# Graph network kernel: TensorE's addresses of a group in one row, read by one load behind the last sum

## What is computed

```python
deg = maximum(segment_sum(ones, dst, n), 1)          # first network, 3 steps
for _ in range(3):
    msg = silu(concat([h[src], h[dst], edge_attr]) @ W1e + b1e) @ W2e + b2e
    agg = segment_sum(msg, dst, n) / deg
    h = h + silu(concat([h, agg]) @ W1n + b1n) @ W2n + b2n
x = layernorm(x + h)
for W, root, b in layers:                            # second network, 3 layers, relu between
    seg = edge_type * n + dst
    agg = segment_sum(h[src], seg, 4 * n) / maximum(count, 1)
    h = h @ root + b + einsum('rni,rio->no', agg, W)
out = layernorm(x + h)
```

## Time and profile before

| | us |
|---|---|
| median of 3 runs | 6185.32 |
| lowest, highest | 6181.42, 6193.58 |
| profiled execution | 6186.73 |
| its span | 6184.7 |
| busy in it: TensorE, DVE, POOL, ACT | 4992.0, 3707.7, 3328.4, 2689.5 |

### The profile page before, as it was taken

How to read it: one execution, slowest core, us unless ns; L and a number is a source line. 1 busy time by engine, 2 the same in 40 slices (tenths; PEclk the granted TensorE clock), 3 DMA queues, 4 the chain that set the end, 5 groups by cost and what they waited for, 6 DMA issues and landing times.

```text
span 6184.7 us, 171993 instructions
## 1 busy us (share of the span) xinstructions
PE 4992.0 (81%) x47650; PEld 4584.0 (74%) x47651; DVE 3707.7 (60%) x9362; ACT 2689.5 (43%) x4966; POOL 3328.4 (54%) x4176
## 2 busy tenths in 40 slices
PE   3666666631888888888888888889999999999998
PEld 2444444421777776888878888879998999989997
DVE  6444444421777775555545555478885888768885
ACT  1111111112556565555545555555553555545553
POOL 1777777740555553444434444446663666636663
PEclk9999965555899998999989999999997999989997
DMA  8111111148899995666646666624442444324441
GB/s 311 29 29 29 29 29 29 29 117 260 282 291 305 301 305 188 220 221 220 221 153 224 221 222 221 201 92 132 132 132 72 133 133 132 128 79 133 132 132 58
DMA packets 358208, 975.40 MB, mean 158 GB/s; under 512 B 70911, under 2 KB 83539, under 8 KB 358154
## 3 DMA queue, kind: packets, MB, share of 16 engines
q1 hardware_dynamic: 317096, 946.00, 46.4%
q0 software_dynamic: 38400, 28.13, 2.6%
q10 hardware_dynamic: 2658, 0.51, 0.0%
HBM read 774.54 MB, written 199.05 MB: 157 GB/s over the span
## 4 chain that ended last, share of the span: by engine, by line
PE 67%; POOL 14%; issue 11%; DMA 4%; another core or an unknown queue 2%; DVE 2%; ACT 0%; POOLq 0%; SPq 0%; ACTq 0%; DVEq 0%
PE sums L902 20%; PE sums L897 15%; POOL recs L510 13%; PE gat L871 11%; PE gat L872 11%; PE gat L875 6%; DMA arena<-recs 2%; DMA recs<-arena 2%; PE gat L994 1%; PE gat L992 1%; PE sums L1005 1%; DVE arena L1149 0%; PE gat L794 0%; PE gat L976 0%
## 5 line engine op out<-in xcount | busy, mean ns | idle before, releaser
L523 POOL TENSOR_SCALAR arena<-iota_f,arena 128x128 f32<-128x128 f32 x1920 | 1210.5, 647 | 1471.1 <-PE sums L897 1285.2
L871 PE MATMUL gat<-table,arena 128*128 x7680 | 1945.3, 254 | 28.6 <-issue 12.8
L872 PE MATMUL gat<-table,arena 128*128 x7680 | 1945.5, 254 | 0.0
L902 PE MATMUL sums<-arena 128*128 128x192 bf16 x15360 | 1887.1, 246 | 0.0
L1293 DVE TENSOR_SCALAR arena<-iota_s,meta_t 128x512 bf16<-128x512 int16 x3840 | 1525.5, 470 | 360.6 <-PE sums L902 360.6
L897 PE MATMUL sums<-arena 128*128 128x64 f32 (+1 forms) x7680 | 1020.3, 278 | 414.1 <-issue 410.4
L902 PEld LDWEIGHTS sums<-arena 128*128 128x128 bf16 x15360 | 1325.2, 98 | 0.1
L897 PEld LDWEIGHTS sums<-arena 128*128 128x128 f32 x7680 | 946.4, 195 | 460.9 <-issue 459.9
L510 POOL DMA_INDIRECT recs<-arena x800 | 952.4, 1190 | 377.1 <-issue 372.2
L662 ACT CAST arena<-gat 128x768 bf16<-128x768 f32 x960 | 767.1, 799 | 808.5 <-PE gat L872 808.5
L648 ACT ACTIVATE arena<-iota_f,arena 128x128 f32<-128x128 f32 x1920 | 613.5, 390 | 953.7 <-PE sums L897 952.8
(11 more groups left out here) (184 smaller groups left out, 4760.6 us busy)
## 6 DMA issues: line engine op xcount, KB each, us to landing
arena<-hots_d SPq DMA_DIRECT2D x320, 768.0 KB, 5.2
arena<-hots_d SPq DMA_DIRECT2D x480, 512.0 KB, 3.4
arena<-recs SPq DMA_DIRECT2D x640, 272.0 KB, 3.0
hots_d<-arena SPq DMA_DIRECT2D x160, 768.0 KB, 7.2
arena<-rows_d SPq DMA_DIRECT2D x160, 512.0 KB, 6.4
recs<-arena SPq DMA_DIRECT2D x1, 43520.0 KB, 119.2
recs<-arena POOLq DMA_INDIRECT x800, 2.9
arena<-in_edge_attr_dram SPq DMA_DIRECT2D x100, 62.5 KB
```

The lines of the kernel that those rows point to most:

```text
L523: ins = pool.tensor_scalar(oh[u % 2][:, j, :], iota_f[:], rec_in[u][:, j, PLACE:PLACE + 1], None, ALU.is_equal)
L871: pe.matmul(at, ohT[u][:, 0, tile], table_flat[:, bass.ds(off[j], K3)], start=True, stop=False)
L872: ins = pe.matmul(at, ohT[u][:, 1, tile], table_next[:, bass.ds(off[j], K3)], start=False, stop=l >= LAYERS)
L902: ins = pe.matmul(accp[s][:, 256 * r:256 * r + K3], oh4[u][:, t, r * P:(r + 1) * P], gb[u][:, t, :], start=t == 0, stop=t == GT - 1)
```

## The change

The tile columns and the three numbers of a group are put in one row of 11 words (`ROW = GT + 3`) of a tensor `places` on partition 0: eight tile columns, destination column, sum column, place in `acc`. SP first writes `off_i` to `offs_d` in DRAM, waits, and reads it back into the rows. In stretches 0 to 2 one TENSOR_LOAD of ten words replaces the three, and it stands behind the last sum of the stage instead of the first. The sum column is loaded with the gather of its own group and used two stages later, so it has four registers. In stretches 3 to 5 the load keeps eight words and its place, and reads them from the row. POOL's word comes from the row.

```diff
--- before.py
+++ after.py
@@ -50,6 +50,7 @@
     CH = -(-NB // 4)
     ROOTS = -(-NB // 8)
     LAYERS = 3
+    ROW = GT + 3
     HC = 32
     POOL_HOTS = GT // 2
     CHUNKS = EC // HC
@@ -57,6 +58,7 @@
 
     recs = nc.dram_tensor("recs", [NT * P, REC], F32, kind="Internal").ap()
     ends_d = nc.dram_tensor("ends_d", [1, KEYS], F32, kind="Internal").ap()
+    offs_d = nc.dram_tensor("offs_d", [1, NT], I32, kind="Internal").ap()
     rows_d = nc.dram_tensor("rows_d", [2, NT, P], BF16, kind="Internal").ap()
     hots_d = nc.dram_tensor("hots_d", [NG, P, 3 * GT * P], BF16, kind="Internal").ap()
     hots_by_group = hots_d.rearrange("g p w -> p g w")
@@ -122,8 +124,9 @@
         inv_cnt = sb("inv_cnt", [P, NB, R])
         stat = sb("stat", [P, 4, NB])
         meta_t = sb("meta_t", [P, NT, 4])
-        offsets = sb("offsets", [1, NT + GT], I32)
-        goff = sb("goff", [1, (NG + 1) * 3], I32)
+
+        places = sb("places", [1, (NG + 1) * ROW], I32)
+        places_v = places[:].rearrange("a (g w) -> a g w", w=ROW)
 
 
         WORDS = 27200
@@ -296,6 +299,7 @@
         ends_stored = sem("ends_stored")
         ends_in = sem("ends_in")
         tables_made = sem("tables_made")
+        offs_stored = sem("offs_stored")
         tables_in = sem("tables_in")
         hots_made = sem("hots_made")
         hots_turned = sem("hots_turned")
@@ -406,8 +410,11 @@
                 for s in range(2):
                     load_attr(2 * i + s, s)
             sp.wait_ge(tables_made, 2)
-            sp.dma_start(offsets[0:1, 0:NT], off_i[:]).then_inc(tables_in, 16)
-            sp.dma_start(goff[0:1, 0:3 * NG], goff_i[0:GP, :, :].rearrange("g j w -> g (j w)")).then_inc(tables_in, 16)
+            sp.dma_start(offs_d.rearrange("a (q c) -> (a q) c", c=TP), off_i[:]).then_inc(offs_stored, 16)
+            sp.wait_ge(offs_stored, 16)
+            sp.dma_start(places_v[0:1, 0:NG, 0:GT], offs_d.rearrange("a (g j) -> a g j", j=GT)
+                         ).then_inc(tables_in, 16)
+            sp.dma_start(places_v[0:1, 0:NG, GT:ROW], goff_i[0:GP, :, :]).then_inc(tables_in, 16)
 
             for s in range(2):
                 sp.wait_ge(rec_stored[s], 16 * GT * (EG // 2))
@@ -535,7 +542,7 @@
                     for u in range(4):
                         m = k * NG + 4 * i + u
                         reg = pool.alloc_register(f"acc_at{k}_{u}")
-                        pool.load([reg], goff[0:1, bass.ds(3 * (4 * i + u) + 2, 1)])
+                        pool.load([reg], places[0:1, bass.ds(ROW * (4 * i + u) + GT + 2, 1)])
                         to = pool.snap(reg, min_val=0, max_val=R * HID * (NB - 1))
                         pool.wait_ge(acc_read, done(m))
                         pool.wait_ge(added, done(m - 1))
@@ -814,7 +821,7 @@
             pe.wait_ge(tables_in, 32)
             tile_regs = [[pe.alloc_register(f"tile_off{s}_{j}") for j in range(GT)] for s in range(2)]
             dst_reg = [pe.alloc_register(f"dst_off{s}") for s in range(2)]
-            sum_reg = [pe.alloc_register(f"sum_off{s}") for s in range(2)]
+            sum_reg = [pe.alloc_register(f"sum_off{s}") for s in range(4)]
 
             for l in range(2 * LAYERS):
                 if 0 < l < LAYERS:
@@ -843,16 +850,13 @@
                     pe.wait_ge(turn_out, CH * (2 + k))
                     pe.wait_ge(x_split, k + 1)
 
-                def load_gather(g, u, l=l):
-
-                    pe.load(tile_regs[u % 2], offsets[0:1, bass.ds(GT * g, GT)])
+                def load_places(g, u, l=l):
+
                     if l < LAYERS:
-                        pe.load([dst_reg[u % 2]], goff[0:1, bass.ds(3 * g, 1)])
-
-                def load_sums(g, u, l=l):
-
-                    if l < LAYERS:
-                        pe.load([sum_reg[u % 2]], goff[0:1, bass.ds(3 * g + 1, 1)])
+                        pe.load(tile_regs[u % 2] + [dst_reg[u % 2], sum_reg[u % 4]],
+                                places[0:1, bass.ds(ROW * g, GT + 2)])
+                    else:
+                        pe.load(tile_regs[u % 2], places[0:1, bass.ds(ROW * g, GT)])
 
                 def gather_ready(g, u, i, l=l):
                     if l == 0:
@@ -915,36 +919,24 @@
                             dst_off = pe.snap(dst_reg[u % 2], min_val=0, max_val=ROWW * (NB - 1) + K3)
                         gather_ready(g, u, i)
                     if adds and l < LAYERS:
-                        to = pe.snap(sum_reg[u % 2], min_val=0, max_val=512 * (BANKS - 1) + REC * (PER_BANK - 1))
-                    def next_places():
+                        to = pe.snap(sum_reg[(u + 2) % 4], min_val=0, max_val=512 * (BANKS - 1) + REC * (PER_BANK - 1))
+                    for j in range(GT):
                         if gathers:
-                            load_gather(g + 1, u + 1)
-                        if not known or 1 <= g <= NG:
-                            load_sums(g - 1, u + 1)
-
-                    if l < LAYERS:
+                            gather_tile(g, u, j, off, dst_off)
+                        if adds and l >= LAYERS:
+                            if j == 0:
+                                sums_ready(g - 2, (u + 2) % 4)
+                            sums_tile(g - 2, (u + 2) % 4, j, to)
+                            if j == 3 and gathers:
+                                load_places(g + 1, u + 1)
+                    if adds and l < LAYERS:
+                        sums_ready(g - 2, (u + 2) % 4)
                         for j in range(GT):
-                            if gathers:
-                                gather_tile(g, u, j, off, dst_off)
-                        for j in range(GT):
-                            if adds:
-                                if j == 0:
-                                    sums_ready(g - 2, (u + 2) % 4)
-                                sums_tile(g - 2, (u + 2) % 4, j, to)
-                            if j == 0:
-                                next_places()
-                    else:
-                        for j in range(GT):
-                            if gathers:
-                                gather_tile(g, u, j, off, dst_off)
-                            if adds:
-                                if j == 0:
-                                    sums_ready(g - 2, (u + 2) % 4)
-                                sums_tile(g - 2, (u + 2) % 4, j, to)
-                            if j == 3:
-                                next_places()
-
-                load_gather(0, 0)
+                            sums_tile(g - 2, (u + 2) % 4, j, to)
+                    if gathers and (l < LAYERS or not adds):
+                        load_places(g + 1, u + 1)
+
+                load_places(0, 0)
                 for g in range(4):
                     stage(g, g, 0)
                 with pe.Fori(1, QUADS) as i:
@@ -1023,8 +1015,7 @@
             for t in (xn[:, NB - 1, :], we8[:], w2e[:], table[:, NB:SPAN * NS, :, :, :]):
                 dve.memset(t, 0.0)
             dve.memset(eps[:], EPS)
-            dve.memset(offsets[0:1, NT:NT + GT], 0)
-            dve.memset(goff[0:1, 3 * NG:3 * NG + 3], 0)
+            dve.memset(places[:], 0)
             dve.memset(zeros_b[:], 0.0)
             dve.memset(ones_e, 1.0)
             step(dve.memset(block_step[:], float(REC)))
```

## The result

| | before | changed |
|---|---|---|
| median of the runs, us | 6184.76 | 7028.98 |
| lowest to highest | 6181.42 to 6193.58 | 7020.2 to 7038.48 |
| ratio, 95% interval | | 1.1363, 1.1343 to 1.1382 |
| span of the profiled execution | 6184.7 | 7018.2 |

What follows compares the result with a forecast made beforehand. The sequencer's three loads a stage were taken to bound stretches 0 to 2, the array 3 to 5. 268 us (stretches 1 and 2) plus 66 (stretch 0), 334 off 6186.7, gave 5853, as median 5851 us; range 5775 to 5945.

Steps and rivals of the forecast that it cites:

- What bounds the kernel: Stretches 0 to 2 run at the sequencer's pace, its three loads in a row starving the array; 3 to 5 at the array's.
- Two loads fewer: In 480 stages, dropping two one-word loads saves 0.95 us, the longer load adds 0.083: 0.867 us less sequencer time a stage.
- My upper bound: Worst case for the ten-word load: as long as the eight-word load plus two single loads of 0.30 us.
- The load's new place: Behind all eight sums, 1.81 us of array work covers the 0.68 us load and some 0.5 us more; array not dry.
- Stretch 0: Sequencer's stage falls from 5.364 to 4.50 us, but DMA binds at 4.95: gain 66 us, bounds 0 and 139.
- My doubt about loads of up to 1836 ns: Stretch 0's eight-word load took a median of 912, up to 1836 ns, unexplained; noted in favour of the slower rival.
- Stretches 3 to 5: Sequencer's stage of 3.6 us keeps its slack against the array's 3.96, with the same eight-word load: gain 0.
- Setup: SP's added DMA and wait cost a few us against 60 of cover: 0, or some 3 us once without cover.
- The rival that came true: All stretches: rows starting every 44 bytes, not 32, lengthen loads; 6296 us if the eight-word load doubled; chance 0.03.
- its own formula: Eight-word load x longer: stretches 0 to 2 gain 0.867 - 1.25 x a stage; 3 to 5 forgive about 0.24 us.
- Loads that hold nothing up: Rival: matmuls are pushed while a load runs, so the lost 0.87 us has another cause; 6185 us, chance 0.02.
- the 303 GB/s that I took for near the end: Stretch 0's DMA rate at 0.92 busy; a stage's 1.59 MB would take 5.25 us at it, 4.83 at share 1.0.

Runs made afterwards that it cites:

- the moved rows: The kernel before, its rows of eight moved up by one word, so each starts 4 bytes behind a multiple of 32: 7532.0 us, one run.

## Why the prediction was wrong

*What bounds the kernel* was right for stretches 1 and 2: with one load of 0.85 us they went from 4.8 to 4.07. The stages of the earlier trace rows were up to 0.06 us off, since their windows missed a few loads.

*Two loads fewer* was right in what it removed and wrong in what it added, and this is **the step that failed: "from one word (305 ns) to eight (595) is 41 ns a word, so ten words take 0.68 us"**. I drew a line through two points which both start on 16 bytes and took its slope for the price of a word. But eight words behave as two accesses, not eight, and ten took 1.08 us at best and 2.40 in three groups of four. All points now, in us:

| words | start on 16 bytes | elsewhere |
|---|---|---|
| 1 | 0.30 | 0.30 |
| 8 | 0.59 | 1.94 |
| 10 | 1.08 | 2.40 |
| 12 | 0.85 | |

Eight to twelve is one block more, 0.26; eight to ten is two words more, 0.49; off the start, two words more cost 0.46. Blocks and accesses are a model that fits these durations, and it foretold the one for twelve words (0.86) and the ones of the moved rows (1.94); no trace shows an access. My upper bound, "eight plus two single loads of 0.30 at worst", 1.19 us, was sound for an aligned row and did not hold the other case.

The Trainium skill (Runtime: NRT & Kernel Launch, Instruction fetch mechanics) gives some 200 ns a register for such loads, even in bulk. That page of the Trainium skill (Terms) has them from HBM, and I did not use it; by its figure ten words would have been an estimated 2 us. Unaligned loads here come near it (0.24 us a word), aligned ones do not (0.07 to 0.11). The Trainium skill (Advanced Engine Details and Errata, SBUF Cachelines) has lines of 16 bytes in SBUF, which fits the block of four words.

*The load's new place* was right for a short load: no cost in stretches 1 and 2, whether with the loads of before or with twelve words. With loads of 2.40 us the array did run dry behind the sums.

*Stretch 0*: DMA was named as next, at 4.95 us a stage. With twelve words it is at 4.81 and a share of 0.97. The price was nearly right; the changed kernel never came near it, with loads of 3.12 us on average there. My doubt about loads of up to 1836 ns there was a sign that a load's time is not a count of words, and I left it at that.

*Stretches 3 to 5* were put at 0: "same load, same place, eight words". Same in everything but the start of the row. They cost 356 us.

*Setup* held: the copies were issued at 1274.5 and 1275.1 against 1272.5 and 1273.2.

*The rival that came true* was the fourth, with its mechanism ("the old row of eight started every 32 bytes, the new one every 44") and its point right: slower from an eight-word load of 1.09 us; three of four took 1.94. Its price stopped at a doubling, 6296 us. With the mean of the eight-word load, 1.60 us, its own formula gives about 6740, and 366 us of loss in stretches 3 to 5, near the 356 measured; most of the rest up to 7029 is stretch 0, which lost 254 us where the formula has 62. I gave this rival 3 in 100 (with "two thirds of it slower" the chance of "slower" should have been 2, not 3) because one-word loads take 305 ns from any address. That is no evidence: one word is one access wherever it lies.

*Loads that hold nothing up* stayed ruled out: in the stage shown above no matmul started between the last sum and the end of the load. The rule of the Trainium skill (Advanced Engine Details and Errata, Sequencer Loop) that the prediction weighed, by which instructions are read and queued while a control instruction executes, stays contradicted for TENSOR_LOAD here.

## What to carry to other kernels

Where a table in SBUF is read into registers, put each row on a multiple of 16 bytes and read whole blocks of four words, also if two are padding: 12 aligned words are cheaper than 10, and 8 unaligned words cost over three times 8 aligned ones. When a change merges small reads into one, look first at what it does to the address of the reads that stay, and take no slope from points that share a property which the change gives up. A sequencer that reads registers holds up every matmul behind it, so its time belongs into the sum of a stage like the array's.

## What the runs showed that I had not expected

- The price of a TENSOR_LOAD by its start: 0.59 or 1.94 us for the same eight words.
- Loads of registers that grow in stretch 0, with the mean of twelve words at 1.37 us instead of 0.85; in one run each, stores from SBUF did a little of it, loads into SBUF at 374 to 385 GB/s none. The rest has no known cause.
- A clock that falls with the loads: with 1.94 us in every stage the array had a granted clock of 0.76 in stretch 1, against 0.97 before and 1.00 with the load of twelve words.
- DMA rates beyond the 303 GB/s that I took for near the end: 334 in stretch 0 at a share of 0.97, and 385 where all traffic is loads.
